# A node table of 28 fine places by 448 rows, and ten and eleven picked tiles in turn, in a graph network kernel

## The reference

```python
def _nnconv(x, src, dst, edge_attr, ew, eb, rw, rb):
    W = (edge_attr @ ew + eb).reshape(edge_attr.shape[0], x.shape[1], rw.shape[1])
    xj = x[src]
    msg = jnp.einsum('ei,eio->eo', xj, W)
    agg = jax.ops.segment_sum(msg, dst, num_segments=x.shape[0])
    return agg + x @ rw + rb
```

## Time and profile before

| | |
|---|---|
| median of three runs | 7418.35 us |
| span of the profiled execution | 7417.2 us |
| the median less that span | 1.15 us |
| TensorE busy | 7176.4 us (97%) |
| VectorE busy | 5854.1 us (79%) |
| GpSimd busy | 5325.5 us (72%) |
| ScalarE busy | 4977.4 us (67%) |
| mean granted clock of TensorE | 0.980 of full speed |

### The profile page before, as it was taken

The page is one execution under the profiler, slowest core; times in us unless marked ns, Lnnn a source line. Parts: engine busy times, 40 slices in busy tenths (PEclk is TensorE's granted clock), DMA queues, the critical chain, the costliest instruction groups (busy, mean ns, idle before and its releaser), DMA issues.

```text
span 7417.2 us, 138584 instructions
## 1 busy us (share of the span) xinstructions
PE 7176.4 (97%) x53192; PEld 6600.5 (89%) x53192; DVE 5854.1 (79%) x7566; ACT 4977.4 (67%) x8367; POOL 5325.5 (72%) x5635
## 2 busy tenths in 40 slices
PE   4999999999999899999999999989999999999998
PEld 2999999999999799999999999979999999999998
DVE  4888888887878788788878788778878788788875
ACT  3666666666676566666666666656666666666665
POOL 4777777777777377777777777747777777777773
PEclk7999999999999899999999999989999999999998
DMA  8121112111111111211211111111212211111111
GB/s 41 31 31 31 31 30 31 31 31 31 31 30 31 27 31 31 31 31 31 31 31 30 31 31 31 31 28 31 31 30 31 31 31 31 32 31 29 31 32 22
DMA packets 783276, 229.34 MB, mean 31 GB/s; under 512 B 643869, under 2 KB 733869, under 8 KB 782619
## 3 DMA queue, kind: packets, MB, share of 16 engines
q1 hardware_dynamic: 529252, 172.27, 11.1%
q0 software_dynamic: 180000, 46.44, 8.2%
q10 hardware_dynamic: 73367, 1.76, 1.0%
HBM read 216.52 MB, written 3.52 MB: 30 GB/s over the span
## 4 chain that ended last, share of the span: by engine, by line
PE 84%; DVE 8%; issue 4%; DVEq 3%; DMA 1%; ACT 0%; ACTq 0%
PE bank L1077 69%; PE bank L1044 10%; DVE xbig L641 3%; DVEq L722 3%; PE bank L1092 1%; DVE agg L727 1%; DVE spread L686 1%; PE bank L1091 1%; PE bank L1102 1%; DVE agg L595 1%; PE bank L1104 1%; DMA key_all<-in_src 1%; PE bank L1149 1%; PE bank L1161 1%; DVE xg L691 0%
## 5 line engine op out<-in xcount | busy, mean ns | idle before, releaser
L471 POOL DMA_INDIRECT xg<-node_table,idx x5625 | 5324.6, 947 | 1995.6 <-issue 1784.6
L1077 PE MATMUL bank<-nodes,low_hot 128*128 128x400 f32 x30000 | 5743.3, 348 | 79.1 <-DVE spread L686 52.8
L1077 PEld LDWEIGHTS bank<-nodes,low_hot 128*128 128x128 f32 x30000 | 5404.4, 188 | 289.2 <-issue 190.1
L917 ACT ACTIVATE distance<-key_all,low_id 128x640 bf16<-128x640 int16 x3000 | 2242.9, 818 | 1909.7 <-issue 1219.6
L686 DVE TENSOR_TENSOR spread<-mask,bank 128x400 f32<-128x400 uint8 x3750 | 1991.5, 566 | 1233.4 <-PE bank L1077 1232.3
L923 ACT ACTIVATE low_hot<-distance,one 128x640 fp32r<-128x640 bf16 x3000 | 2233.0, 817 | 0.0
L691 DVE TENSOR_REDUCE xg<-spread 128x80 f32<-128x2000 f32 x750 | 1677.1, 2236 | 25.7
L641 DVE TENSOR_TENSOR xbig<-xg,bank 128x1280 f32<-128x1280 f32 x750 | 1327.5, 1810 | 1.0 <-issue 0.2
L1044 PE MATMUL bank<-xbig,hot 128*32 128x144 f32 x18750 | 994.7, 295 | 0.1
L1044 PEld LDWEIGHTS bank<-xbig,hot 128*32 128x32 f32 x18750 | 820.9, 109 | 162.0 <-issue 99.1
L633 DVE TENSOR_TENSOR hot<-bank,dst_rel 128x800 f32<-128x800 f32 x375 | 367.9, 981 | 0.0
(11 more groups left out here) (109 smaller groups left out, 939.8 us busy)
## 6 DMA issues: line engine op xcount, KB each, us to landing
key_all<-edge_keys SPq DMA_DIRECT2D x375, 320.0 KB, 3.7
xg<-node_table,idx POOLq DMA_INDIRECT x5625
ea<-in_edge_attr SPq DMA_DIRECT2D x375, 100.0 KB
idx<-in_src SPq DMA_DIRECT2D x375, 7.5 KB
node_table<-rows_room SPq DMA_DIRECT2D x3, 781.2 KB
xbig<-node_table SPq DMA_DIRECT2D x9, 192.0 KB
xbig<-in_x SPq DMA_DIRECT2D x2, 781.2 KB
xbig<-in_dst ACTq DMA_DIRECT2D x1, 782.5 KB, 68.6
```

The source lines that it names most:

```text
L471: pool.indirect_dma_start(out=xg[u][:, j, :], out_offset=None, in_=table[:, :], in_offset=bass.IndirectOffsetOnAxis(ap=idx[u][:, j:j + 1], ...
L917: nc.scalar.activation(distance[f][:, 0:tiles.stop - tiles.start, :], key[u % KEYS][:, tiles, :], ACT.Abs, bias=low_id[:, f:f + 1]).then_i ...
L1077: last = nc.tensor.matmul(p_sel[t % BANKS], low_hot[:, f, t, :], nodes[i][:, f, :, :].rearrange("p d f -> p (d f)"), start=(f, i) == (0, 1 ...
```

## The change

The node number is split another way: by division by 28 into a row (448 of them) and a fine place (28). 448 rows are three and a half folds. The half fold is held twice, in partitions 0 to 63 as the upper part and in 64 to 127 as the lower part, and `low_id` gives the same rows to both, so a single matmul adds both. A tile then takes seven matmuls of 448 columns (`PASSES`) in place of eight of 400. The table in HBM gets 44 rows of padding, written once, and is loaded with one row of 28 x 16 numbers a run.

Groups with an even number pick ten tiles and fetch 15; those with an odd number pick eleven and fetch 14. The tile slots are numbered 0 to 10, and a group of ten uses slots 1 to 10, so its halves are slots 1 to 5 and 6 to 10, those of a group of eleven 0 to 5 and 6 to 10. Keys are computed from sources that are loaded one run of 1920 numbers a group, in float arithmetic with a correction, before the transposes, and only the fine places are transposed. The banks go round by the count of all picks. Some buffers share room with others (`bn_s`, `col_i`, `far_zT`, `far_zxT`).

```diff
-PICKED = 10
-FETCHED = TILES - PICKED
+PICKS = (10, 11)
+MOST = max(PICKS)
 FOLD = 4
-FOLD_BITS = 2
+FINE = 28
+ROWS = 448
+PASSES = 2 * FOLD - 1
...
-PARTS = (slice(0, 5), slice(5, 10))
-HALF = 5
+HALF = MOST - 5
...
+    HALF_P = P // 2
+    PLACES = FINE * ROWS
+    assert SELW <= 512 and PLACES >= N and 2 * ROWS == PASSES * P
+
+    table = nc.dram_tensor("node_table", [PLACES, D], F32, kind="Internal").ap()
+    keys = nc.dram_tensor("edge_keys", [G, MOST * P], I16, kind="Internal").ap()
...
+    def picks(g):
+
+        return PICKS[g % len(PICKS)]
+
+    def fetches(g):
+
+        return TILES - picks(g)
+
+    def first_pick(g):
+
+        return MOST - picks(g)
+
+    def parts(g):
+
+        return slice(first_pick(g), HALF), slice(HALF, MOST)
...
-        nodes = [sb(f"nodes{i}", [P, FOLD, D, FINE], F32R) for i in range(2)]
+        nodes = sb("nodes", [P, PASSES, D, FINE], F32R)
...
-                sp.wait_ge(s_tail, layer + 1)
-                whole = N // P
-                by_block = table[0:whole * P, :].rearrange("(m p) d -> p m d", p=P)
-                for k in range(FOLD):
-                    count = len(range(k, whole, FOLD))
-                    sp.dma_start(nodes_raw[:, k, 0:count, :], by_block[:, k::FOLD, :]).then_inc(s_nload, 16)
-                sp.dma_start(nodes_raw[0:N - whole * P, whole % FOLD, whole // FOLD, :],
-                             table[whole * P:N, :]).then_inc(s_nload, 16)
+                sp.wait_ge(s_padw, 16)
+                by_row = table.rearrange("(r f) d -> r (f d)", f=FINE)
+                whole = (FOLD - 1) * P
+                sp.dma_start(nodes_raw[:, 0:FOLD - 1, :, :].rearrange("p k f d -> p k (f d)"),
+                             by_row[0:whole, :].rearrange("(k p) x -> p k x", p=P)).then_inc(s_nload, 16)
+                for i in range(2):
+                    sp.dma_start(nodes_raw[i * HALF_P:(i + 1) * HALF_P, FOLD - 1, :, :].rearrange("p f d -> p (f d)"),
+                                 by_row[whole:ROWS, :]).then_inc(s_nload, 16)
...
+                g = b * SLOTS + u
+                sp.dma_start(key[u % KEYS][:, first_pick(g):MOST, :].rearrange("p t e -> p (t e)"),
+                             keys[g:g + 1, first_pick(g) * P:MOST * P].to_broadcast([P, picks(g) * P])).then_inc(s_key[u], 16)
...
+            sp.wait_ge(s_pad, 1)
+            sp.dma_start(table[N:PLACES, :], pad[:]).then_inc(s_padw, 16)
...
-                        for j in range(FETCHED):
+                        for j in range(fetches(b * SLOTS + u)):
...
+            twin = slice(HALF_P, P), slice(FOLD - 1, FOLD)
+            nc.vector.tensor_scalar(low_id[twin], low_id_i[twin], -1.0, float(HALF_P), ALU.mult, ALU.add)
...
-            dve.wait_ge(s_src, 32)
-            step(nc.vector.tensor_scalar(src_int, src_pick, 7 + FOLD_BITS, None, ALU.logical_shift_right))
-            step(nc.vector.tensor_copy(fine[:].rearrange("p (g j) -> p g j", g=G), src_int))
-            step(nc.vector.tensor_scalar(src_int, src_pick, P * FOLD - 1, None, ALU.bitwise_and))
-            nc.vector.tensor_copy(key_f, src_int).then_inc(s_keyf, 1)
-            for c in range(PICKED):
-                dve.wait_ge(s_keyT, c + 1)
-                nc.vector.tensor_copy(key16[:, c, :], bank[c % 2][0:G, 0:P]).then_inc(s_key16, 1)
+            dve.wait_ge(s_src, 16)
...
+            for tiles, numbers, j in spans:
+                last = nc.vector.tensor_scalar(cells(place.bitcast(I32), tiles, j), numbers, 1.0 / FINE, 0.5 / FINE - 0.5,
+                                               ALU.mult, ALU.add)
+            step(last)
+            step(nc.vector.tensor_scalar(fine_f, place.bitcast(I32), float(FINE), None, ALU.mult))
...
+            for c in range(-(-MOST // GANG)):
+                some = min(GANG, MOST - c * GANG)
+                dve.wait_ge(s_fineT, c + 1)
+                nc.vector.tensor_copy(fine[:, :, c * GANG:c * GANG + some].rearrange("p g t -> p t g"),
+                                      bank[c][:, 0:some * G].rearrange("p (t g) -> p t g", g=G)).then_inc(s_fine, 1)
...
-                upper, lower = (nodes[i][:].rearrange("p k d f -> p k f d") for i in (1, 0))
-                nc.vector.tensor_copy(upper, nodes_cut)
-                nc.vector.tensor_tensor(lower, nodes_raw, nodes_cut, ALU.subtract).then_inc(s_nodes, 1)
+                by_place = nodes[:].rearrange("p k d f -> p k f d")
+                lower, upper = (by_place[:, i:PASSES - 1:2, :, :] for i in (0, 1))
+                nc.vector.tensor_copy(upper, nodes_cut[:, 0:FOLD - 1, :, :])
+                nc.vector.tensor_copy(by_place[0:HALF_P, PASSES - 1, :, :], nodes_cut[0:HALF_P, FOLD - 1, :, :])
+                nc.vector.tensor_tensor(lower, nodes_raw[:, 0:FOLD - 1, :, :], nodes_cut[:, 0:FOLD - 1, :, :], ALU.subtract)
+                nc.vector.tensor_tensor(by_place[HALF_P:P, PASSES - 1, :, :], nodes_raw[HALF_P:P, FOLD - 1, :, :],
+                                        nodes_cut[HALF_P:P, FOLD - 1, :, :], ALU.subtract).then_inc(s_nodes, 1)
...
             def take_picks(layer, b, u, half):
 
 
                 k = layer * G + b * SLOTS + u
-                t0, t1 = PARTS[half].start, PARTS[half].stop
+                part = parts(k % G)[half]
+                t0, t1 = part.start, part.stop
+                before = picks_before(k)
                 dve.wait_ge(s_mask, k + 1)
                 dve.wait_ge(s_xg, k * 2 + half)
                 for t in range(t0, t1):
-                    dve.wait_ge(s_pick, k * PICKED + t + (1 + PICKED))
+                    n = before + t - first_pick(k % G)
+                    dve.wait_ge(s_pick, n + 1)
                     nc.vector.tensor_tensor(
                         spread[:, t - t0, :, :],
                         mask[k % PAIR][:, t, :].unsqueeze(1).to_broadcast([P, D, FINE]),
-                        p_sel[t % BANKS].rearrange("p (d f) -> p d f", d=D), ALU.mult).then_inc(s_taken, 1)
-                dve.wait_ge(s_taken, k * PICKED + (t1 + PICKED))
-                nc.vector.tensor_reduce(xg[u % SLOTS][:, FETCHED + t0:FETCHED + t1, :],
+                        p_sel[n % BANKS].rearrange("p (d f) -> p d f", d=D), ALU.mult).then_inc(s_taken, 1)
+                dve.wait_ge(s_taken, n + 1)
+                nc.vector.tensor_reduce(xg[u % SLOTS][:, TILES - MOST + t0:TILES - MOST + t1, :],
                                         spread[:, 0:t1 - t0, :, :], AX_X, ALU.add).then_inc(s_xg, 1)
...
-            for i in range(PICKED // RUN):
-                act.dma_start(src_pick[:, :, i * RUN:(i + 1) * RUN],
-                              src_b.rearrange("(g a) p j -> a p g j", a=BLOCKS)[FETCHED // RUN + i, :, :, :]
-                              ).then_inc(s_src, 16)
+            act.dma_start(src_rows, src.rearrange("(g e) -> g e", g=G)[:, GE - SOURCES:GE]).then_inc(s_src, 16)
...
+                tiles = parts(k % G)[half]
                 act.wait_ge(s_key[u], body * 16 + 16)
 
-                act.wait_ge(s_pick, k * PICKED + tiles.stop)
+                if k:
+                    act.wait_ge(s_pick, picks_before(k - 1) + parts((k - 1) % G)[half].stop - first_pick((k - 1) % G))
...
             def pick(layer, b, u, t):
 
                 k = layer * G + b * SLOTS + u
-                for half, tiles in enumerate(PARTS):
+                for half, tiles in enumerate(parts(k % G)):
                     if t == tiles.start:
                         pe.wait_ge(s_low, k * 2 + (half + 1 + 2 * CREDIT))
 
-                before = t - BANKS if t >= BANKS else max(range(t, PICKED, BANKS)) - PICKED
-                pe.wait_ge(s_taken, k * PICKED + (before + 1 + PICKED))
-                for f in range(FOLD):
-                    for i in (1, 0):
-                        last = nc.tensor.matmul(
-                            p_sel[t % BANKS], low_hot[:, f, t, :],
-                            nodes[i][:, f, :, :].rearrange("p d f -> p (d f)"),
-                            start=(f, i) == (0, 1), stop=(f, i) == (FOLD - 1, 0))
+                place_in_all = picks_before(k) + t - first_pick(k % G)
+                if place_in_all >= BANKS:
+                    pe.wait_ge(s_taken, place_in_all - BANKS + 1)
+                for i in range(PASSES):
+                    last = nc.tensor.matmul(
+                        p_sel[place_in_all % BANKS], low_hot[:, i // 2, t, :],
+                        nodes[:, i, :, :].rearrange("p d f -> p (d f)"), start=i == 0, stop=i == PASSES - 1)
                 last.then_inc(s_pick, 1)
...
-                for t in range(PICKED):
+                for t in range(first_pick(0), MOST):
...
-                            if not (last and u == SLOTS - 1):
+                        for t in range(MOST):
+                            if not (last and u == SLOTS - 1) and t >= first_pick(g + 1):
                                 pick(layer, b, u + 1, t)
                             if t in (1, 3) and t // 2 < len(ended):
                                 transpose_round(layer, ended[t // 2])

```

(47 more changed lines are left out.)

112 lines of the change are left out of this document (54 added, 58 removed).

## The result

| | before | after |
|---|---|---|
| time, median of 4 runs beside each other | 7418.73 us | **7701.9 us** (7699.77 to 7704.84) |
| ratio to before, 95% interval | | 1.0381 [1.0369, 1.0394] |
| profiled execution: time, span | 7418.35, 7417.2 us | 7701.39, 7698.5 us |
| mean granted clock of TensorE | 0.980 | 0.970 |
| first sums of a layer to the sums of its last group but one | 2312.8, 2313.9, 2313.5 us | 2409.8, 2407.8, 2409.6 us |

The change costs 3.8%, 283 us. The forecast was 7620, in a range from 7400 to 7690: the direction is as predicted, the time lies 82 us above the forecast and 12 above the range. The last line of the table shows where it went: 97.0 + 93.9 + 96.1 = 287 us inside the three layers (the last group of a layer, with no picks of a next one beside it, takes some 7 us in both).

The account below looks back on a forecast made before the run. TensorE's own work was taken as the bound, with two stalls on VectorE in each fourth group. 7417.2 + 105 (picks) + 105 (stall) - 9 (start and turns) = 7618, forecast 7620 us, range 7400 to 7690.

Parts of the forecast that it names:

- What bounds the kernel: TensorE's own work sets the end, with two stalls on VectorE in each fourth group; GpSimd is the near rival.
- the wait for agg: Sign in TensorE's timeline: the round after the additions would wait some 2 us for VectorE's additions to agg.
- Pick matmuls: On TensorE, 448 columns take 202.1 ns against 182.1 for 400; with 10.5 tiles, +1.1 us for four groups, +105 us.
- rival (4): The pick matmuls' surcharge grows with columns: 204.0 ns each, 60.0 us instead of 59.4, total 7675 us; chance 15%.
- the wait for the additions: After every fourth group TensorE's round waits for VectorE; stall from 1.2 to 2.3 us, +1.1 us 93 times, +105 us.
- the end of the second one: The second wait after a fourth group, of the fifth pick for a bank, would be gone.
- What is covered: GpSimd (0.6 us less a group), ScalarE (+1.1 us each second group) and VectorE's added work stay hidden behind TensorE.
- rival (3): GpSimd sets the pace, 18.73 us a group against TensorE's 18.81; 375 x 0.62 us won, 7180 us; chance 2%.
- Start and turns: Layer starts and turns: faster source load -12 us, table split +1 us for each of three, together -9 us.

Follow-up runs that it names:

- e3: The changed kernel with seven useless matmuls of 448 columns ahead of the round that waits for the additions; 7615.34 us, 1.0268 of before.
- e1: The changed kernel with rounds counted from the group's first pick, so two picks stand ahead of the wait for the additions; 7573.72 us, 1.0208 of before.
- e2: The changed kernel with ten picked tiles in every group and the round two picks behind the sums; 7326.36 us, 0.9876 of before.
- e4: The kernel before, with only the rounds moved to behind the first and third pick instead of the second and fourth; 7541.97 us, 1.0168 of before.
- e8: The changed kernel with ten picks a group, nine in each twelfth, rounds counted from the first pick and VectorE's places read early; 7340.02 us, 0.9894 of before.

## Why the prediction was right in direction and 82 us short

The whole of the difference of spans is 7698.5 - 7417.2 = 281 us. What the runs give for it: picks +147, clock +87, stall +62, the rest of the layers -9, start -11, turns +4, end +1.

- **What bounds the kernel.** Right. TensorE's own work set the end before and after, and the wait for agg grew where it was said to.
- **Pick matmuls: 202.1 ns taken, 203.6 measured.** Too small. 42 x 7 x 203.6 - 40 x 8 x 182.15 ns = 1.57 us for four groups instead of 1.1, +147 us instead of +105. The prediction took the 15.4 ns above the columns' own time as the same for each matmul; in the means they grow with the columns (13.1 ns at 300, 16.9 at 448), nearly as rival (4) had it (204.0).
- **The step that failed: the wait for the additions.** "Only one pick stands ahead of the wait, not two" was right, and so were the place of the wait and the end of the second one. It was priced as time lost while TensorE stands, +105 us. The stall gave some 62: 41 are e3 less e1, the pick that no longer stands ahead of the wait, and 21 are there with two picks ahead as well, for in e1 the group of the additions takes 1.47 us more than the common group of ten (19.14 - 17.67), where before it took 1.24 (19.24 - 18.00), 93 times. Without a fall of the clock the stall is 1.94 us (e3, 19.61 - 17.67) where the prediction had 2.3. A part of the reason can be read in VectorE's timeline after:

```profile
3478.63 0.44 DVE L730 TENSOR_TENSOR mask<-bank,fine 128x280 uint8<-128x280 f32 x1
...
3479.49 1.79 DVE L789 TENSOR_TENSOR agg<-agg,bank 16x100 f32 x5 [0.43 <-issue]
```

The gap ahead of the additions is 0.43 us instead of 0.72: it took in the longer reduction, and the round comes 5.97 us behind the sums, 5.93 before (3439.59 - 3433.66). The prediction had named this gap as possible cover and then not counted it. What it had no term for was what the standstill does to the clock: in 50 places the picks that follow run at 1.2 GHz for 3.4 us, 373 ns a matmul instead of 204. e3 prices that at 87 us. So this step cost 149 us where 105 were taken, with the stall 43 too large and the clock missing; that the total came within 82 us owes something to the first error, which is luck. The total fell short by the picks (42 us) and by this step (44), start and turns add 3, and the rest of the layers, which no run assigned, takes 9 off.
- **What is covered.** ScalarE and GpSimd are covered, as said. GpSimd now waits 530 us (29.8 before), until a group's features are loaded, and no product waits for a gather. VectorE's work grew by 606 us, 1.6 a group, as taken, and TensorE waits for its takes 6.3 us in all. What the prediction said of GpSimd, "it is GpSimd that is carried by a lead", was more true than I used: rival (3) was argued from 18.73 against 18.81, and e2 runs at 18.57.
- **Start and turns.** The targets land at 79.36 us, 92.32 before, and the first pick begins at 137.69, 152.36 before: -14.7 where -12 was taken. It gives -11 at the first sums, and the turns +4 and the end +1 where +3 was taken: -6 instead of -9.
- **The range.** Its upper end took in rival (4) and the forecast's stall, and no second-order cost of a longer standstill. The Trainium skill tells of such a cost (TensorE: Matmul & The Clock Gate, A second HAM failure mode: psum-queue depth-cycling): in a kernel measured there TensorE went idle for small pieces of time between groups of matmuls, often enough that its clock went to and fro between the two levels, and throughput fell by it. This trace agrees, with 50 falls at waits of 1.7 to 2.1 us.

Still open: why 50 of the 90 waits come with the fall and 40 of the same length do not (43 of 90 in e4, with waits of 1.6 to 2.0 us; none in e3, where the wait left is 0.7 us at most); and the 9 us in the layers.

## What to carry to other kernels

A stall on TensorE has two prices, the time that it stands and the clock that it may lose afterwards; so count the work queued ahead of a wait whenever a loop's indices are shifted, and if it can't be kept, fill the hole with work. Price a change of a matmul's columns by two sizes of the same instruction, not by one size and a constant. And an engine whose work per step is as long as the bound's is no bound while it has a lead: look at what it waits for at the turn of the stages and divide that by the number of steps. But e8, priced from such a lead, was 100 us out: the first waits for its product show where the lead ends.

## What the hardware showed unasked

- TensorE's pace for one instruction is not one number. The same 63 pick matmuls behind a round take 12.87 us or 13.27 (both in the timeline after, at full clock), 6 ns a matmul apart for the whole stretch, each in about half of the stretches. What chooses between them no run shows.
- The cost above a matmul's columns is seen only at 2.4 GHz: at 1.2 GHz pick matmuls of 400 columns start every 333 ns and those of 448 every 373 (median of 362 in the stretches at half clock after), just their columns.
- A useless matmul can be worth more than it costs: 90 x 7 of them, in time that was idle anyway, brought 87 us.
